# A Hadamard product by a 128-block: sums and differences on GpSimd, products interleaved with transposes

## The reference, cut to what matters

```python
bias = braak_embed[braak_stages][..., None]          # one number per row of x
q    = x + bias
attn = softmax(einsum('bsd,btd->bst', q, f))
y    = einsum('bst,btd->bsd', attn, f)
xh   = y @ H                                         # H: 256x256 Hadamard matrix / 16
s    = max(max|xh| over the row, 1e-5) / 7
xq   = clip(round(xh / s), -8, 7) * s
wq   = ternary(weight) * mean|weight| of its row
out  = x + einsum('bsi,oi->bso', xq, wq)
```

## Time and profile before

| | |
|---|---|
| time, 3 runs | 109.68, 109.69, 110.32 us (median 109.69) |
| profiled execution | 109.14 us; its span, first to last instruction, is 107.3 us |
| PE busy | 98.1 us (91%), 801 matmuls |
| PEld busy | 91.2 us (85%) |
| DVE busy | 91.1 us (85%), 233 instructions |
| ACT busy | 66.9 us (62%) |
| POOL busy | 56.0 us (52%) |
| mean granted TensorE clock | 0.984 of full speed |
| chain that ended last | PE 59%, DVE 27%, ACT 7% of the span |

### The profile page before, as it was taken

How to read it: one execution, slowest core, us unless ns; L and a number is a source line. 1 busy time by engine, 2 the same in 40 slices (tenths; PEclk the granted TensorE clock), 3 DMA queues, 4 the chain that set the end, 5 groups by cost and what they waited for, 6 DMA issues and landing times.

```text
span 107.3 us, 2555 instructions
## 1 busy us (share of the span) xinstructions
PE 98.1 (91%) x801; PEld 91.2 (85%) x801; DVE 91.1 (85%) x233; ACT 66.9 (62%) x172; POOL 56.0 (52%) x64
## 2 busy tenths in 40 slices
PE   5989999999999999999999999999999998989420
PEld 2559899899999999899999899999899998968300
DVE  1187599799989999999899999999999999598780
ACT  5047877674857677585846684848576675473710
POOL 4006899703654745383837374747538444045350
PEclk9999999999999999999999999999999999999985
DMA  1988523225277636527382529382722222210214
GB/s 71 281 308 251 184 80 101 102 52 191 49 247 107 237 105 205 146 102 241 109 233 98 195 49 228 114 292 50 279 63 98 49 98 49 98 66 31 98 49 147
DMA packets 14702, 14.90 MB, mean 139 GB/s; under 512 B 7906, under 2 KB 8680, under 8 KB 14696
## 3 DMA queue, kind: packets, MB, share of 16 engines
q1 hardware_dynamic: 14684, 14.82, 45.0%
q10 hardware_dynamic: 12, 0.00, 0.0%
HBM read 8.92 MB, written 4.19 MB: 122 GB/s over the span
## 4 chain that ended last, share of the span: by engine, by line
PE 59%; DVE 27%; ACT 7%; issue 3%; DVEq 0%; ACTq 0%
PE xh_bank L432 16%; PE score_bank L432 15%; PE fh_bank L432 7%; PE prob_bank L421 5%; DVE raw_scale L723 4%; PE f_bank L421 4%; PE out_bank L487 4%; PE q_bank L421 4%; DVE scaled L735 4%; DVE abs_max L716 3%; DVE prob_lo L749 3%; PE out_bank L389 3%; ACT prob L618 3%; DVE q_lo L749 2%; DVE neg_max L776 2%
## 5 line engine op out<-in xcount | busy, mean ns | idle before, releaser
L321 POOL TENSOR_TENSOR result<-scaled,x_all 128x512 f32<-128x512 f32 x13 | 16.6, 1277 | 22.7 <-DVE scaled L735 22.7
L313 POOL TENSOR_TENSOR code<-code,magic 128x512 bf16<-128x512 f32 x13 | 13.5, 1040 | 11.8 <-ACT code L596 11.8
L305 POOL TENSOR_TENSOR q_nat<-x_all,bias 128x512 f32 (+1 forms) x15 | 15.6, 1039 | 7.5 <-DMA x_all<-x_dram 7.5
L612 ACT CAST fh_hi<-fh_bank 128x512 fp32r<-128x512 f32 x16 | 9.4, 587 | 15.6 <-PE fh_bank L432 15.6
L618 ACT ACTIVATE prob<-score_bank,neg_max 128x256 f32<-128x256 f32 x32 | 14.9, 475 | 2.1 <-DVE neg_max L776 2.1
L596 ACT ACTIVATE code<-xh_bank,inv_scale 128x256 f32<-128x256 f32 x30 | 12.7, 478 | 5.3 <-DVE inv_scale L728 5.3
L587 ACT CAST f_hi<-f_bank 128x512 fp32r<-128x512 f32 x16 | 9.4, 586 | 8.0 <-PE f_bank L421 8.0
L432 PE MATMUL score_bank<-f_hi,q_hi 128*128 128x256 f32 x64 | 14.0, 300 | 0.3 <-ACT prob L618 0.3
L432 PE MATMUL fh_bank<-had,f_hi 128*128 128x256 f32 x64 | 14.2, 303 | 0.0
L432 PE MATMUL xh_bank<-fh_hi,prob_hi 128*128 128x256 f32 x60 | 12.5, 290 | 0.5 <-DVE prob_lo L749 0.2
L432 PE MATMUL score_bank<-f_hi,q_lo 128*128 128x256 f32 x64 | 12.8, 282 | 0.0
(11 more groups left out here) (100 smaller groups left out, 226.5 us busy)
## 6 DMA issues: line engine op xcount, KB each, us to landing
f_nat<-f_dram SPq DMA_DIRECT2D x16, 256.0 KB, 2.8
x_all<-x_dram SPq DMA_DIRECT2D x16, 256.0 KB, 3.0
out_dram<-result SPq DMA_DIRECT2D x14, 256.0 KB, 2.0
had_raw<-hadamard_dram SPq DMA_DIRECT2D x1, 256.0 KB, 3.7
w_raw<-weight_dram SPq DMA_DIRECT2D x1, 256.0 KB, 4.9
out_dram<-result SPq DMA_DIRECT2D x2, 128.0 KB, 1.7
out_dram<-scaled SPq DMA_DIRECT2D x1, 256.0 KB, 2.0
code_t<-code SPq DMA_TRANSPOSE x13, 2.5
```

Source lines behind the costliest of these rows:

```text
L305: nc.gpsimd.tensor_tensor(q_nat[:, b.k], x_all[:, b.at].rearrange("p (t d) -> p t d", t=T), bias[:, b.at].unsqueeze(2).broadcast_to([P, T, ...
L313: nc.gpsimd.tensor_tensor(as_rows(code16[:, b.k]), as_rows(code), magic[:, :].broadcast_to([P, W]), ALU.subtract).then_inc(code16_ready, 1)
L321: nc.gpsimd.tensor_tensor(result[:, b.k], as_rows(scaled[:, b.k]), x_all[:, b.at], ALU.add).then_inc(result_ready, 1)
```

## The change

H's form is used. With h the 128-block, f @ H is [(f1+f2) h, (f1-f2) h], where f1 and f2 are the column halves of f. The changed kernel makes g = [f1+f2, f1-f2] on GpSimd (`f_turned`) and transposes g where it transposed f; x with bias goes through the same sum and difference (q_nat), and the score q·f is then half of q'·g, the factor 0.5 being put into the split of q (`scale=0.5`). The Hadamard product becomes 8 products of 128 columns with h alone, and TensorE issues them one by one, each behind one transpose of f or q. The bias is added on ScalarE (`add_bias`, to the lower half, doubled). The residual result is made one step later, x is loaded three steps ahead instead of two, and `row_scales` uses two `tensor_scalar` in place of one `scalar_tensor_tensor`.

```diff
+        def sum_and_difference(engine, to, of, first):
+
+            low, high = halves(of)
+            engine.tensor_tensor(to[:, :, 0:P], first[:, :, 0:P], high, ALU.add)
+            return engine.tensor_tensor(to[:, :, P:D], low, high, ALU.subtract)
...
@@ gpsimd, step
+                if b := batch(LAG_STORE):
+                    wait(pool, scaled_ready, b.at + 1)
+
+                    wait(pool, stored[b.k], 16 * b.half)
+                    nc.gpsimd.tensor_tensor(
+                        result[:, b.k], as_rows(scaled[:, b.k]),
+                        x_all[:, b.at], ALU.add).then_inc(result_ready, 1)
+
                 if b := batch(-1):
+                    wait(pool, f_loaded[b.k], 16 * b.half + 16)
+                    wait(pool, f_in_bank, b.at - 1)
+                    sum_and_difference(nc.gpsimd, f_turned[:, b.k], f_nat[:, b.k], f_nat[:, b.k]
+                                       ).then_inc(f_sum_ready, 1)
                     wait(pool, x_loaded[b.k], 16 * b.half + 16)
+                    wait(pool, x_biased_ready, b.at)
                     wait(pool, q_in_bank, b.at - 1)
-                    nc.gpsimd.tensor_tensor(
-                        q_nat[:, b.k], x_all[:, b.at].rearrange("p (t d) -> p t d", t=T),
-                        bias[:, b.at].unsqueeze(2).broadcast_to([P, T, D]), ALU.add
-                    ).then_inc(q_ready, 1)
+                    sum_and_difference(nc.gpsimd, q_nat[:, b.k], x_tiles(b), x_biased[:, b.k]
+                                       ).then_inc(q_ready, 1)
...
@@ tensor
+            def hadamard_one(b, n):
+
+                (t, c), low = divmod(n // 2, C), n % 2
+                return pe.matmul(fh_bank[:, t, c * P:(c + 1) * P],
+                                 (f_lo if low else f_hi)[:, b.k, c, t * P:(t + 1) * P], had[:, :],
+                                 start=not low, stop=bool(low))
...
+            def turns_with_hadamard(b_load, b_fh):
+
+                wait(pe, f_sum_ready, b_load.at + 1)
+                wait(pe, f_lo_ready, b_load.at)
+                wait(pe, fh_lo_ready, b_fh.at)
+                for n in range(C * T):
+                    turned = turn_one(f_bank, f_turned[:, b_load.k], n)
+                    if n == C * T - 1:
+                        turned.then_inc(f_in_bank, 1)
+                    hadamard_one(b_fh, n)
+                wait(pe, q_ready, b_load.at + 1)
+                wait(pe, q_lo_ready, b_load.at)
+                for n in range(C * T):
+                    turned = turn_one(q_bank, q_nat[:, b_load.k], n)
+                    if n == C * T - 1:
+                        turned.then_inc(q_in_bank, 1)
+                    mm = hadamard_one(b_fh, C * T + n)
+                mm.then_inc(fh_in_bank, 1)
...
             def step(batch):
-                for stage, lag in STAGES_IN_ORDER:
-                    if b := batch(lag):
-                        stage(b)
+                turns_with_hadamard(batch(LAG_LOAD_TURN), batch(LAG_SCORE))
+                turn_prob(batch(LAG_MIX))
+                score(batch(LAG_SCORE))
+                times_ternary(batch(LAG_OUT))
+                mix(batch(LAG_MIX))
...
@@ scalar
+            def add_bias(b):
+
+                wait(act, x_loaded[b.k], 16 * b.half + 16)
+                wait(act, q_ready, b.at - 1)
+                for t in range(T):
+                    a = nc.scalar.activation(x_biased[:, b.k, t], x_all[:, b.at, t * D:t * D + P],
+                                             ACT.Identity, bias=bias[:, b.at, t:t + 1])
+                a.then_inc(x_biased_ready, 1)
+
             STAGES_IN_ORDER = (
                 (split_f, LAG_LOAD_TURN), (split_q, LAG_LOAD_TURN), (quantize, LAG_QUANT),
-                (split_prob, LAG_MIX), (split_fh, LAG_SCORE),
+                (split_prob, LAG_MIX), (split_fh, LAG_SCORE), (add_bias, -2),
                 (exponentials, LAG_SCORE))
...
@@ vector
-                nc.vector.scalar_tensor_tensor(
-                    out=raw_scale[:, :], in0=abs_max[:, :], scalar=1.0 / POS,
-                    in1=least_scale[:, b.k], op0=ALU.mult, op1=ALU.max
-                ).then_inc(raw_scale_ready, 1)
+                for t in range(T):
+                    v = nc.vector.tensor_scalar(raw_scale[:, t:t + 1], abs_max[:, t:t + 1], 1.0 / POS,
+                                                least_scale[:, b.k, t:t + 1], ALU.mult, ALU.max)
+                v.then_inc(raw_scale_ready, 1)
...
@@ sync, ahead of the steps
+            sp.wait_ge(q_ready, 1)
+            sp.dma_start(x_all[:, 2], x_dram[2]).then_inc(x_loaded[0], 16)
```

More of the change, by code:

```diff
@@ L471, in times_hadamard @@
                 wait(pe, fh_lo_ready, b.at)
-                product(fh_bank, [(f_hi[:, b.k], had), (f_lo[:, b.k], had)]).then_inc(fh_in_bank, 1)
+                for n in range(2 * C * T):
+                    mm = hadamard_one(b, n)
+                mm.then_inc(fh_in_bank, 1)
             def mixed(b):
@@ L529, in _ @@
             mix(b0)
[L530 to L534 removed]
+            turns_with_hadamard(Batch(0, 3), b2)
+            turn_prob(b1)
+            score(b2)
+            weights()
+            mix(b1)
             pe.wait_ge(tern_t_ready, 1)
@@ L664, in _ @@
                 step(peeled(i))
-            with act.Fori(LOOP_FROM, B // 2) as half:
+            with act.Fori(LOOP_FROM, B // 2 - 1) as half:
                 for odd in range(2):
                     step(looped(half, odd))
+            for i in range(B - 2, B):
+                step(peeled(i))
             third_last, second_last, last = (Batch(0, B - n) for n in (3, 2, 1))
```

85 lines of the change are left out of this document (49 added, 36 removed).

## The result

The changed kernel takes **123.11 us** (median of 4 runs, 123.03 to 123.37) against 110.0 us (109.68 to 111.13) for the kernel before on the same chip: a ratio of 1.118, 95% interval 1.109 to 1.126. It is slower, by 12% where 8% was forecast; the time lies in the range, 4.2 us above the forecast of 118.9.

A forecast was written before the change was run, and what follows sets the result against it. PE bounds the kernel before; a ring through fh_lo was to bound the changed one. Start 25.2, 11 steps of 6.26 (68.9) and end 22.4 give span 116.5; 1.84 and 0.55 more give 118.9 us, range 115.5 to 124.0.

The forecast's parts named there:

- ring through fh_lo: Each step: fh_lo, PE's pairs, q_hi, code, prob, VectorE's scales, fh_lo again; claimed to set the step at 6.26 us.
- the formula: Step length of the fh_lo ring: 4.64 us from q_hi to fh_lo's end, plus 0.41, plus seven pairs.
- Part 1, the pair: On PE, one transpose plus one 128-column product: 0.173 us, against 0.227 with 256 columns.
- The Trainium skill's rule on loads: Load time on PE as columns / 1.2 ns: pair 0.214 us, step 6.55, whole about 122.4; set aside for the trace.
- Part 2, the ring: Wait for fh_lo moved to PE's first instruction closes a ring: 4.64 + 1.62 = 6.26 us a step.
- The hand-over: From fh_lo's end to q_hi besides seven pairs: hand-overs 0.04 each, transposes behind a wait 0.06, eighth transpose's record 0.27 us.
- The stretch from q_hi to the end of fh_lo: ACT and DVE part of the ring: 4.64 us from the trace, claimed unchanged.
- Part 3, GpSimd hidden: GpSimd's sums, subtraction and result: 5.2 us of work in a step of 6.26, claimed to fit, its waits hidden.
- Part 4, raw_scale: VectorE's raw_scale as two tensor_scalar: 0.11 to 0.15 us longer, not on the ring; collisions with POOL go.
- POOL blocks VectorE's small instructions: Rival: POOL blocks several VectorE instructions each step beyond the slack, up to 0.7 us a step, 126 us; chance 0.04.
- Part 5, start and end: Weights' signs on POOL end at 22.9, step 4 starts at 25.2 instead of 22.47; the end kept at 22.4 us.
- The rival with a pair of 0.22: Products of 128 columns on PE stream no faster: step 6.59 us, time 122.9 us; chance 0.17.

The follow-up runs named there:

- e1: Changed kernel with the Hadamard product and its wait for fh_lo back in their old place, not interleaved with transposes: 115.36 us, ratio 1.041, steps of 5.67 us.
- e3: Changed kernel with a second PSUM bank for fh, so the product waits for fh_lo of one batch earlier: 115.53 us, ratio 1.048, steps of 5.98 us.
- e2: Kernel before with only the interleaving: its 256-column Hadamard products each behind one transpose, wait for fh_lo in front, no GpSimd sums: 123.19 us, ratio 1.113.
- e7: Changed kernel with the halved products in their old place, the weights' signs a step later and least_scale as two 128x1 instructions: 111.9 us, ratio 1.013.
- e5: Kernel before with only raw_scale written as two TENSOR_SCALARs of 128x1: 107.44 us against 109.96, ratio 0.975, steps of 5.56 us.
- e10: Changed kernel with two transposes, then two halved products, four times, in place of one and one, eight times: 123.49 us, ratio 1.120.
- e4: Changed kernel with least_scale as two instructions of 128x1 in place of one of 128x2: 121.87 us, ratio 1.104, steps of 6.54 us.
- e9: Changed kernel with f transposed ahead of the wait for fh_lo and two halved products behind each q transpose: 123.2 us, ratio 1.117, steps of 6.62 us.
- e12: Changed kernel with f transposed before the fh_lo wait, two products behind each q transpose, least_scale as two 128x1 instructions: median 118.04 us, steps of 6.10 us.

## Why the prediction was right, and where it was too low

The forecast was slower, by a ring through fh_lo, with steps of 6.26 us. The direction holds, and so does the mechanism, as one of two: a second ring of nearly the same length, through GpSimd, was not in it. e1 and e3 take the ring away in two different ways and lose 1.0 and 0.7 of the 1.0 us per step with it; e2 builds it into the kernel before and gets it at the length that the formula gives.

**Part 1, the pair: mis-sized.** The term was 7 x 0.173; the pair is 0.197, so 7 x 0.197 = 1.38 instead of 1.21, **0.17 us** a step. The step that failed is the price of the changeovers, 0.11 to 0.118 behind a transpose and, "If 128 columns stream in half of the 256 columns' time", 0.055 to 0.06 behind a product. In the rows the product starts 0.05 behind its transpose and the next transpose 0.14 to 0.15 behind the product. One behind another, the halved products stand 0.112 us apart in e7, like transposes, and those of 256 columns 0.118. So halving the columns saves next to nothing of a product, and e7 and e5, where PE is the busy engine, both have steps of 5.56. Whether it is the stream or the load that keeps the halved product at 0.112 no run separates. The Trainium skill's rule on loads (TensorE: Matmul & The Clock Gate, "LDWEIGHTS"), which would have made the pair 0.214, is nearer to the measured 0.197 than the forecast was, but it stays above it. The 0.197 is also under the sum of two streams (0.109 + 0.112 = 0.221): some overlap is there, 0.024 of the 0.048 that the term had below this sum. e10's group of four at 0.417 is in line with it: one pair, one transpose and one product. What in the changeover takes the rest isn't settled.

**Part 2, the ring: two terms.** The hand-over was taken as 0.04 + 0.06 + 0.27 + 0.04; with the pairs as measured, fh_lo's end to q_hi is 1.80 and 1.86 us in turn, so 0.01 to 0.07 more. The stretch from q_hi to the end of fh_lo, "4.64 us ... Nothing in this stretch is changed", is 4.93 and 4.77 us (67.12 to 72.05, 73.91 to 78.68). This sentence is wrong: no instruction in the stretch is changed, but one of them, least_scale, is held up by an engine beside it, 0.44 and 0.27 us for 0.15, which are, to 0.01, the 0.29 and 0.13 that the stretch is longer. Mean **0.20**. In e4 with that gone the stretch is 4.69 (71.78 less 67.09). The sum: 6.26 + 0.17 + 0.04 + 0.20 = 6.67, measured 6.69. Looked at from the other side, it is GpSimd's ring that sets 6.69, and least_scale's delay is how it slows the first. The forecast ring by itself is e4's 6.54.

**Part 3, GpSimd hidden: right in its size, wrong in its conclusion.** 5.2 us were forecast for it and 5.04 are shown, in a step with room for them. "It fits" was asked of its work alone. Since its subtraction stands where VectorE's small instruction comes, and its result waits for what VectorE does behind that, it had a ring of its own, as long as the step.

**Part 4, raw_scale: right.** Its two instructions take 201 to 215 ns each and are never held up, in this kernel and in e5. Both together take 0.33 us where one took 0.16, 0.17 more for the 0.11 to 0.15 of the forecast. The Trainium skill (SBUF — State Buffer, "Who interferes with whom"), by which tensor_scalar may be blocked, was set aside, and for one column the runs agree with that; for least_scale's two columns they agree with the skill. The rival "POOL blocks VectorE's small instructions" was given 0.04 and up to 0.7 us a step; it is true in kind, at 0.15 in this kernel (e4) and 0.52 in e9's (6.62 against e12's 6.10).

**Part 5, start and end: right in their sum.** Step 4 was forecast at 25.2 and begins at 25.07; PE waits for tern until 22.64, 22.9 was forecast. The wait itself is 2.06 us and not 4.0, since PE comes to it at 20.6 and not at 18.87: step 3 begins later and has the pairs in it. That costs nothing, because the signs set the end. The end was kept at 22.4, measured 22.5.

So the 4.2 us are 11 steps of 0.43, 4.7, and 0.5 less around the span, since the median lies 0.06 above the profiled execution and not 0.55. The rival with a pair of 0.22, at 122.9 us, gives nearly the measured time, but by luck: the pair is 0.17 of the 0.43, and most of the rest is the held-up least_scale.

## What to carry to other kernels

Before interleaving work to overlap two engine phases, follow the new wait back through every in-order queue: a wait moved to the front of a step, on a single buffer that another engine's last instruction frees, makes a ring of everything in between, whose length and not the work saved sets the step. That half the columns are half the time has to be seen in rows first; here a product of 128 took 0.112 us and one of 256 0.118. And when an engine that had room gets more work, ask which small instructions of its neighbour will now fall beside it: writing one of VectorE's 128x2 scalings, raw_scale, as two of 128x1 was worth 2.5% (1.8 to 3.2) on the kernel before, without anything else.

## What the runs showed of the hardware

- A VectorE TENSOR_SCALAR of 128x2 that began while a GpSimd instruction ran ended 23 to 29 ns behind that instruction, in all twelve such cases of the changed kernel, and took up to 0.98 us for it (0.99 in e3, 1.24 in e9) where it takes 0.15. Only the instruction under way counted: in e1 least_scale was let go between the last sum and the subtraction (61.43).
- The SCALAR_TENSOR_TENSOR of 128x2 on the kernel before took 1.03 to 1.04 us in the three cases in which it began 16 to 22 ns behind the start of GpSimd's addition, and 0.16 in the six in which it began 34 to 77 ns ahead of it.
- TENSOR_SCALARs of 128x1 were never held up: 131 to 146 ns in all 64 cases of e4 and e12, raw_scale's pairs 201 to 216 ns. Nor were RECIPROCALs of 128x2: 0.15 us for inv_sum beside the same subtraction, 165 to 167 ns for all 16 of inv_scale in the changed kernel, 13 of which lie wholly beside GpSimd's work. So two columns alone don't make an instruction one of those that wait.
- float32r products of 128 and of 256 columns follow one another after 0.112 and 0.118 us. A transpose and a product in turn take 0.197 with 128 columns and 0.231 with 256; two transposes and two products of 128 columns take 0.417.
- PE's idle 2.06 us at the start left the granted clock at 2.4 GHz in the changed kernel. In e1's traced execution an idle time of 2.46 us was followed by over 6 us at 1.2 GHz, up to about 29.7; by their mean clocks this came in three of its four executions.
